# A token-mixing kernel with a second layer norm: a masked copy goes to GpSimd, a normalisation to ScalarE, and the hand-written order of four engines is set anew

## The chip, the cores and the metric

The kernel runs on one core of a Trainium2 chip. That core has five engines with a queue each: TensorE (PE: matmuls, with a separate row PEld for the weight loads that run ahead of them), VectorE (DVE), ScalarE (ACT), GpSimd (POOL), and SyncE (SP), which here only issues DMAs. An engine works its own program in order, and waits at semaphores for the others. The metric is the device time of one whole execution in microseconds (us), as the median of the runs.

## The reference

Input `x` is 2 sequences of 4096 tokens with 512 channels, in float32. What is computed, cut to what matters:

```python
h = layernorm(x)
xx = shift(h) - h                          # the token before, minus this one
lo = tanh((h + xx * time_maa_x) @ maa_w1.T)          # "low rank"
xrg, xwa, xk, xv = h + xx * (lo_g @ maa_w2[g] + time_maa[g])
r, k, v = xrg @ Wr.T, xk @ Wk.T, xv @ Wv.T           # 512x512 projections
g = tanh(xrg @ gate_w1.T) @ gate_w2
w, a, ma, mk, kk = ...                     # gates of low rank, kk normalised per head
s = 0                                      # 16 heads, a 32x32 state each
for t in tokens:
    s = s * w[t] + (s @ kk[t]) * b[t] + v[t] * k[t]
    y[t] = s @ r[t]
y = headnorm(y) * ln_w + ln_b + (r * k * time_faaaa).sum() * v
x = x + (y * g) @ Wo.T
x2n = layernorm(x)                         # the second normalisation
q = round(x2n / (max|x2n| / 127))          # int8 rows
out = x + (q @ weight_q.T) * x_scale * weight_scale + bias
```

## The kernel before, in words

The tokens are cut into 64 tiles of 64 tokens of both sequences (128 rows). The recurrence over tokens is solved in chunks of 32: per head and chunk, score matrices of 32x32 are built, and a triangular system is inverted by powers (three rounds named `power(m, 0..2)`), then by two halves: `half_inverse` and `inverse`, whose result is the tile `tx`. With `tx` two chunks are solved one after the other (`from_values`, `from_state`, `solve_step`, `from_solutions`, with c = 0 in `bank_b` and c = 1 in `bank_a`).

The work is a software pipeline written out by hand. Every engine has a function `tile_step(i)` which lists, in a fixed order, what that engine does for four tiles at a time: `mix` for tile j = i+1 (first layer norm, shift, low rank, mixed inputs), `project` for tile i (keys, values, queries, gates), `solve` for tile m = i-1 (the recurrence), and `finish` for tile n = i-2 (head norm, output projection, second layer norm, quantising, feed-forward). No scheduler or pool decides anything: the order of lines in `tile_step` is the order on the engine, and semaphores (named by the producer, `v_` DVE, `a_` ACT, `g_` GpSimd, `p_` TensorE) tie the engines together. There are 66 steps, of which 63 both project one tile and solve another.

Names that matter below. On TensorE: `queries` (`bank<-xm_rg,w_r`) and `values` (`bank<-xm_v,w_v`), each a projection cut into four blocks of 4 matmuls, which the profile counts as 8 since a float32 matmul is run in two passes; `transposed_input` (`ident,xn`); `low_rank` (`mix,w_maa`); `project_out` (`w_o,yc`), also in four blocks; `power` (`bank_a<-first/pw`, 64 small matmuls on 32x32 tiles); `half_inverse` and `inverse` (the same with narrower right-hand sides); `from_values` (`km,vT`), on 64x64 tiles. On DVE: `half_inverse(m)` ends with the masked copy `tx<-pw,mask_half`; `inverse(m)` adds TensorE's result to it; `shift_mix(j)` makes `xx` and `mix` from the transposed input `xT`, which ACT copies out of PSUM in `front_transposed`; `quantiser(n)` begins with the second normalisation `x2n<-xres,mv,rs`. Of GpSimd's work the multiplications in `weighted_bonus`, `kept_keys`, `undecayed` and `bonus_values`, and the power of -1/2 (`rs`) in `norm2_rstd`, stand near the change.

Of the kernel before, what the change touches and what calls it, by code (L numbers as in the profile page):

```python
# [34 lines left out]
def rwkv_ffn_kernel(nc, a, out):  # L35
# [11 lines left out]
    with ExitStack() as ctx:  # L47
# [73 lines left out]
        def in_spare(groups):  # L121
# [34 lines left out]
        bn2, mv2, rs2 = sb("bn2", [P, 6]), sb("mv2", [P, 2]), sb("rs2", [P, 2])  # L156
        x2n = sb("x2n", [P, C])
# [34 lines left out]
        (v_pl, v_vraw, v_vsum, v_vT, v_qkT, v_rk, v_blT, v_klT, v_pm, v_km, v_e, v_ptT, v_sums, v_te, v_t4, v_tx,  # L192
         v_teT, v_t, v_rhs, v_state, v_rkv) = (
            sem(f"v_{n}") for n in
            "pl vraw vsum vT qkT rk blT klT pm km e ptT sums te t4 tx teT t rhs state rkv".split())
        a_pw, a_u, a_y, a_g, a_b2, a_k2, a_vT2 = (sem(f"a_{n}") for n in "pw u y g b2 k2 vT2".split())
        g_qk, g_qkf, g_rkv = (sem(f"g_{n}") for n in "qk qkf rkv".split())
# [3 lines left out]
        (v_ysqT, v_yvar, v_yrs, v_z1, v_yg, v_x2, v_st2, v_x2n, v_qs, v_q1, v_q2, v_ffn) = (  # L201
            sem(f"v_{n}") for n in "ysqT yvar yrs z1 yg x2 st2 x2n qs q1 q2 ffn".split())
        a_ysq, a_lnv, a_rstd, a_affine, a_qT = (sem(f"a_{n}") for n in "ysq lnv rstd affine qT".split())
# [75 lines left out]
        @block.sync  # L279
        def _(sp):  # L280
            def load_x(i):
                sp.wait_ge(a_xn, count(i, 1, 0))
                for b in range(B):
                    sp.dma_start(xin[b * TB:(b + 1) * TB, :], x_tiles[i, b]).then_inc(x_loaded, 16)

            def load_residual(m):
                sp.wait_ge(stored, count(m, 32, 0))
                sp.wait_ge(g_x2b, count(m, 1, 0))
                sp.wait_ge(v_x2n, count(m, 1, 0))
# [36 lines left out]
        def _(pool):  # L326
# [134 lines left out]
            def tile_step(i, mix=True, project=True, solve=True, finish=True):  # L461
                j, m, n = i + 1, i - 1, i - 2
                if mix:
                    norm_rstd(j)
                if project:
                    kept_keys(i)
                if solve:
                    decayed_state(m)
                    bonus(m)
                if finish:  # L470
                    add_bonus(n)
                if solve:
                    weighted_bonus(m)
                if project:
                    undecayed(i)
                if solve:
                    bonus_values(m)
                if finish:
                    norm2_rstd(n)
                    residual_bias(n)  # L480
                if mix:
                    mixed_inputs(j, XWA, XRG)
                if finish:
                    finish_rows(n)
# [17 lines left out]
        def _(act):  # L502
# [156 lines left out]

            def quantised(n):  # L660
                act.wait_ge(p_qT, count(n, 1, 1))
                run(qT[:], fb[1][:].bitcast(BF16)[:, 0:W].rearrange("p (k t) -> p k t", k=KB),
                    ACT.Copy).then_inc(a_qT, 1)

            def tile_step(i, mix=True, project=True, solve=True, finish=True):
# [8 lines left out]
                if project:  # L674
                    ma_gate(i)
                    a_gate(i)
                    squares(i)
                    mk_gate(i)
# [7 lines left out]
                if solve:  # L686
                    power(m, 1)
                if finish:
                    head_affine(n)
                if solve:  # L690
                    value_pairs(m)
                if project:
                    log_sigmoid(i)
                if mix:
                    normalised(j)
                if solve:
                    power(m, 2)
# [4 lines left out]
                if project:  # L702
                    log_squares(i)
                    exp_tables()
                    key_decay(i)
                    exponentials(i)
                if mix:
                    low_rank(j)
                if project:
                    queries(i)  # L710
                if solve:
                    solution(m, 0)
                    output_gate(m)
                if project:
                    gate_hidden(i)
                if solve:
                    solution(m, 1)
                if finish:
                    quantised(n)
                if mix:  # L720
                    hidden(j, 0)
                    hidden(j, 1)
                if solve:
                    outputs(m, 0)
                    outputs(m, 1)
# [14 lines left out]
        def _(dve):  # L740
# [133 lines left out]
            def half_inverse(m):  # L874
# [7 lines left out]
                dve.wait_ge(v_t4, count(m, 1, 1))  # L882
                tt(tx[:].rearrange("p g (a t) -> p g a t", a=2),
                   pw[:, :, 1, HALF:].unsqueeze(2).to_broadcast([P, G, 2, HALF]),
                   mask_half[:].rearrange("p (a t) -> p a t", a=2).unsqueeze(1).to_broadcast([P, G, 2, HALF]),
                   ALU.mult).then_inc(v_tx, 1)
# [84 lines left out]
            def tile_step(i, mix=True, project=True, solve=True, finish=True):  # L971
# [9 lines left out]
                if solve:  # L981
                    token_major_values(m)
                    enter(m)
                    power(m, 0)
                if project:
                    key_norm(i)
                if mix:
                    norm_shift(j)
                if solve:
                    token_major_keys(m)  # L990
                if finish:
                    head_norm(n)
                if solve:
                    power(m, 1)
                    scores_k(m)
                if finish:
                    gate_heads(n)
                if project:
                    decay_sums(i)
                if solve:  # L1000
                    bonus_rows(m)
# [5 lines left out]
                if solve:  # L1007
                    half_inverse(m)
                    inverse(m)
                if project:  # L1010
                    removal_directions(i)
                if solve:
                    right_hand_sides(m, 0)
                    bonus_sums(m)
                if finish:
                    residual(n)
                if solve:
# [12 lines left out]
                if solve:  # L1030
                    bonus(m)
                if mix:
# [5 lines left out]
                if project:  # L1038
                    decayed(i)
                if finish:  # L1040
# [22 lines left out]
        def _(pe):  # L1063
# [228 lines left out]
            def tile_step(i, mix=True, project=True, solve=True, finish=True):  # L1292
# [11 lines left out]
                if project:  # L1304
                    queries(i, [0])
                    values(i, [0])
                    decay_gate(i)
                if solve:
                    power(m, 1)
                if project:  # L1310
                    queries(i, [1])
                    values(i, [1])
                    values(i, [2])
                    values(i, [3])
                    queries(i, [2])
                if solve:
                    power(m, 2)
                    from_values(m, 0)
                if mix:
                    transposed_input(j)  # L1320
                if project:
                    queries(i, [3])
# [4 lines left out]
                if finish:  # L1327
                    project_out(n, [1])
                    project_out(n, [2])
                if mix:  # L1330
                    low_rank(j)
                if solve:
# [21 lines left out]
                if mix:  # L1354
                    hidden(j, 0)
                    hidden(j, 1)
                if finish:
                    feed_forward(n)

# [52 lines left out]
```

## Time and profile before

| | |
|---|---|
| median of 3 runs | 3238.7 us (3226.87 to 3242.51) |
| the profiled execution's own time | 3244.0 us |
| its span in the trace | 3242.2 us |
| PE busy | 93% of the span |
| PEld busy | 83% |
| DVE busy | 81% |
| ACT busy | 61% |
| POOL busy | 39% |
| share of PE in the chain that ended last | 92% |

The span is the time from the first to the last instruction in the trace; 1.8 us of the execution lie around it. Busy is the share of the span in which an engine had an instruction in work; matmuls overlap each other, so PE's share alone does not say how near it is to its limit. The chain that ended last is followed back from the last instruction to whatever released each step.

### The profile page before, as it was taken

The numbers are of one execution on the slowest core, as the hardware profiler recorded it, in microseconds if no ns is written. First come the engines' busy times: TensorE is split into PE (matmuls) and PEld (weight loads), VectorE is DVE, ScalarE is ACT, GpSimd is POOL, SyncE is SP. The second block draws the span as 40 slices with busy tenths as digits, with TensorE's granted clock in tenths as the row PEclk, the third lists the DMA queues.
The fourth block names the chain that finished last, engine by engine and source line by source line (L and its number), as shares of the span: only waits on it lengthen the run. The fifth ranks groups of instructions, "written<-read, shape, count | busy, mean of one in ns | idle before, by whom it ended". The sixth has DMA issues, their size and how long they took to land.

```text
span 3242.2 us, 182735 instructions
## 1 busy us (share of the span) xinstructions
PE 3029.1 (93%) x84224; PEld 2675.6 (83%) x84224; DVE 2626.5 (81%) x5443; ACT 1974.8 (61%) x3519; POOL 1270.6 (39%) x1161
## 2 busy tenths in 40 slices
PE   6999999999999999999999999999999999999996
PEld 5888888888888888888888888888888888888884
DVE  4788888888888888887888888887888878888875
ACT  3575675665665665755656656656567566566563
POOL 4334334334334344343344343443433434433332
PEclk9999999999999999999999999999999999999998
DMA  3000000000000000000000000000000000000000
GB/s 118 10 23 20 17 23 19 18 20 18 22 20 17 23 20 17 23 20 17 22 20 19 20 17 23 20 17 23 20 17 23 20 17 20 20 20 20 16 17 19
DMA packets 39380, 70.47 MB, mean 22 GB/s; under 512 B 9812, under 2 KB 10836, under 8 KB 38616
## 3 DMA queue, kind: packets, MB, share of 16 engines
q1 hardware_dynamic: 38616, 58.77, 6.8%
q8 instruction: 664, 10.88, 1.4%
q14 instruction: 100, 0.82, 0.1%
HBM read 41.97 MB, written 16.78 MB: 18 GB/s over the span
## 4 chain that ended last, share of the span: by engine, by line
PE 92%; issue 3%; ACT 2%; DVE 2%; POOL 0%; POOLq 0%; ACTq 0%; DVEq 0%
PE bank L1070 30%; PE bank_a L1209 12%; PE bank L1273 8%; PE bank_a L1187 4%; PE bank L1077 4%; PE bank_b L1187 4%; PE bank_b L1244 3%; PE bank_b L1237 3%; PE bank_a L1237 3%; PE bank_a L1244 3%; PE bank_a L1217 2%; PE bank_a L1225 2%; PE bank L1123 2%; PE bank_a L1263 2%; PE bank_b L1263 2%
## 5 line engine op out<-in xcount | busy, mean ns | idle before, releaser
L504 ACT ACT_TABLE_LOAD x383 | 491.4, 1283 | 19.1 <-DVE shift L761 12.2
L1070 PE MATMUL bank<-xm_rg,w_r 128*128 128x128 f32 x2048 | 285.4, 282 | 4.3 <-issue 3.5
L504 ACT ACTIVATE u<-bank_a,parity 128x256 f32<-128x256 f32 x128 | 53.7, 471 | 386.7 <-PE bank_a L1253 386.7
L1209 PE MATMUL bank_a<-pw,w_ffn_int 32*32 32x64 f32 x16384 | 264.6, 216 | 22.0 <-issue 17.2
L1273 PE MATMUL bank<-w_o,yc 128*128 128x512 f32 x512 | 268.9, 626 | 11.0 <-DVE yc L744 9.3
L1209 PEld LDWEIGHTS bank_a<-pw,w_ffn_int 32*32 32x32 f32 x16384 | 239.6, 106 | 41.7 <-issue 21.3
L1070 PEld LDWEIGHTS bank<-xm_rg,w_r 128*128 128x128 f32 x2048 | 248.9, 191 | 26.8 <-issue 15.9
L504 ACT ACTIVATE u<-bank_b,parity 128x256 f32<-128x256 f32 x128 | 53.8, 471 | 342.3 <-PE bank_b L1253 342.3
L1070 PEld LDWEIGHTS bank<-xm_k,w_k 128*128 128x128 f32 x2048 | 241.2, 194 | 12.5 <-issue 3.8
L1070 PE MATMUL bank<-xm_v,w_v 128*128 128x128 f32 x2048 | 250.2, 275 | 0.0
L1070 PE MATMUL bank<-xm_k,w_k 128*128 128x128 f32 x2048 | 241.7, 277 | 3.5 <-issue 3.5
L1070 PEld LDWEIGHTS bank<-xm_v,w_v 128*128 128x128 f32 x2048 | 239.3, 192 | 0.3
L870 DVE STREAM_TRANSPOSE w_ffn_int<-bank_a 128x512 f32<-128x512 f32 x192 | 137.3, 715 | 90.9 <-ACT pw L504 90.3
L399 POOL TENSOR_TENSOR yc<-yc,rkv 128x512 f32<-128x512 f32 x64 | 82.0, 1281 | 321.7 <-ACT yc L504 321.7
L396 POOL TENSOR_TENSOR kept<-ga,gma 128x512 f32<-128x512 f32 x64 | 81.5, 1274 | 311.6 <-ACT ga L504 311.6
L396 POOL TENSOR_TENSOR kkp<-kk,pinv 128x512 f32<-128x512 f32 x64 | 75.3, 1177 | 288.8 <-DVE kk L744 288.8
L396 POOL TENSOR_TENSOR kmod<-kraw,pinv 128x512 f32<-128x512 f32 x64 | 77.1, 1205 | 261.1 <-ACT pinv L504 261.1
L744 DVE TENSOR_TENSOR first<-bank_a,mask_b 128x1024 f32<-128x1024 f32 x64 | 78.4, 1225 | 106.7 <-PE bank_a L1187 106.7
L399 POOL TENSOR_TENSOR o_sb<-o_sb,x2b 128x512 f32<-128x512 f32 x64 | 81.5, 1274 | 199.3 <-DVE o_sb L968 199.3
L1209 PE MATMUL bank_a<-first,w_ffn_int 32*32 32x64 f32 x8192 | 135.0, 215 | 18.7 <-issue 17.7
L396 POOL TENSOR_TENSOR qkT<-qkT,faaaa_T 128x512 f32<-128x512 f32 x64 | 81.4, 1272 | 166.2 <-DVE qkT L914 166.2
L399 POOL TENSOR_TENSOR xm_wa<-xm_wa,xT 128x512 f32<-128x512 f32 x64 | 89.5, 1399 | 128.4 <-DVE xm_wa L779 128.4
(204 smaller groups left out, 8540.4 us busy)
## 6 DMA issues: line engine op xcount, KB each, us to landing
xin<-in_x SPq DMA_DIRECT2D x128, 128.0 KB, 2.7
xres<-in_x SPq DMA_DIRECT2D x128, 128.0 KB
out<-o_sb SPq DMA_DIRECT2D x128, 128.0 KB, 2.4
w_ffn_int<-in_weight_q SPq DMA_DIRECT2D x1, 2048.0 KB, 10.8
w_k<-in_Wk SPq DMA_DIRECT2D x1, 1024.0 KB
w_r<-in_Wr SPq DMA_DIRECT2D x1, 1024.0 KB
w_v<-in_Wv SPq DMA_DIRECT2D x1, 1024.0 KB
w_o<-in_Wo SPq DMA_DIRECT2D x1, 1024.0 KB, 14.2
```

The costliest lines, as they stand in the source:

```text
L396: return nc.gpsimd.tensor_tensor(out_, in0, in1, ALU.mult)
L399: return nc.gpsimd.tensor_tensor(out_, in0, in1, ALU.add)
L504: return nc.scalar.activation(out_, in_, func, **kw)
L870: V.transpose(pt, pairs(bank_a)[:, :, 0, :]).then_inc(v_ptT, 1)
L1070: ins = mm(bank[:, o * n:(o + 1) * n], weights[:, k, o * P:(o + 1) * P], x[:, k].rearrange("p b t -> p (b t)"), start=(k == 0), stop=(k == ...
L1077: ins = mm(bank[:, o * TOK:(o + 1) * TOK], weights[:, o * P:(o + 1) * P], hidden[:], start=True, stop=True)
L1187: ins = mm(bank[q, 64 * n:64 * n + 64], both(keys_[q, g]), both(aq[q, g, 0:2]), start=True, stop=True)
L1209: ins = mm(bank_a[q, 64 * n:64 * n + 64], pt[q, g, :], source[q, g, 0:2].rearrange("p j t -> p (j t)"), start=True, stop=True)
L1237: mm(bank[q, 4 * CHUNK * j:4 * CHUNK * j + 3 * CHUNK], both(vT2[q, g]), km[q, g].rearrange("p j t -> p (j t)"), start=(j % 4 == 0), stop=F ...
L1244: ins = mm(bank[q, 4 * CHUNK * j:4 * CHUNK * j + 3 * CHUNK], both(s_old2[q, j]), aq[q, g].rearrange("p j t -> p (j t)"), start=False, stop ...
L1263: ins = mm(bank[q, 4 * CHUNK * j + CHUNK:4 * CHUNK * j + 3 * CHUNK], both(u2[q, j]), first[q, g, 2:4].rearrange("p j t -> p (j t)"), start ...
L1273: ins = mm(fb[0][:], yc[:, k * TOK:(k + 1) * TOK], w_o[:, k, :], start=(k == 0), stop=(k == KB - 1))
```

## The change

Two operations change engines. The masked copy `tx<-pw,mask_half` leaves DVE's `half_inverse` and becomes GpSimd's `spread_inverse(m)`; DVE's `inverse` now waits for `g_tx`. The second normalisation leaves DVE's `quantiser` and becomes ACT's `normalised_rows(n)`, as scale times x plus shift; DVE computes the shift (128x1) in a new `norm2_shift(n)`, which waits for GpSimd's `g_rs2`. The other part is the order in `tile_step` of all four engines.

```diff
+            def spread_inverse(m):                                   # GpSimd
+                pool.wait_ge(v_t4, count(m, 1, 1))
+                pool.wait_ge(p_u, count(m, NC, 0))
+                nc.gpsimd.tensor_tensor(tx[:].rearrange("p g (a t) -> p g a t", a=2),
+                   pw[:, :, 1, HALF:].unsqueeze(2).to_broadcast([P, G, 2, HALF]),
+                   mask_half[:].rearrange("p (a t) -> p a t", a=2).unsqueeze(1).to_broadcast([P, G, 2, HALF]),
+                   ALU.mult).then_inc(g_tx, 1)
...
+            def normalised_rows(n):                                  # ScalarE
+                act.wait_ge(v_shift2, count(n, 1, 1))
+                act.wait_ge(v_q2, count(n, 1, 0))
+                run(x2n[:], xres[:], ACT.Identity, scale=rs2[:, 1:2], bias=shift2[:]).then_inc(a_x2n, 1)
...
             def inverse(m):                                          # VectorE
                 dve.wait_ge(p_t, count(m, 1, 1))
-                dve.wait_ge(v_tx, count(m, 1, 1))
+                dve.wait_ge(g_tx, count(m, 1, 1))
...
+            def norm2_shift(n):
+                dve.wait_ge(g_rs2, count(n, 1, 1))
+                dve.wait_ge(a_x2n, count(n, 1, 0))
+                V.scalar_tensor_tensor(shift2[:], mv2[:, 0:1], -1.0, rs2[:, 1:2], ALU.mult,
+                                       ALU.mult).then_inc(v_shift2, 1)
+
             def quantiser(n):
-                dve.wait_ge(g_rs2, count(n, 1, 1))
-                V.tensor_scalar(x2n[:], xres[:], mv2[:, 0:1], rs2[:, 1:2], ALU.subtract, ALU.mult).then_inc(v_x2n, 1)
-                dve.wait_ge(v_x2n, count(n, 1, 1))
+                dve.wait_ge(a_x2n, count(n, 1, 1))
...
                 if finish:                                           # VectorE, tile_step
                     residual(n)
+                    norm2_shift(n)
                 if solve:
                     update_state(m, 0)
...
                 if solve:                                            # TensorE, tile_step
                     power(m, 2)
+                if project:
+                    queries(i, [2])
+                    queries(i, [3])
+                if solve:
                     from_values(m, 0)
                 if mix:
                     transposed_input(j)
-                if project:
-                    queries(i, [3])
                 if finish:
                     project_out(n, [0])
                 if solve:
                     half_inverse(m)
                 if finish:
                     project_out(n, [1])
+                if mix:
+                    low_rank(j)
+                if finish:
                     project_out(n, [2])
-                if mix:
-                    low_rank(j)
```

TensorE, from the last part of `values` ahead of `power(m, 2)` to `inverse(m)`. Before (x4 is one block of `queries` or `values`):

```order
L1070 MATMUL bank<-xm_v,w_v 128x128 x12
L1070 MATMUL bank<-xm_rg,w_r 128x128 x4
L1209 MATMUL bank_a<-pw,w_ffn_int 32x64 x64
L1237 MATMUL bank_b<-km,vT 64x96 x16
L1104 MATMUL bank<-ident,xn 128x128 x4
L1070 MATMUL bank<-xm_rg,w_r 128x128 x4
L1273 MATMUL bank<-w_o,yc 128x512
L1217 MATMUL bank_a<-pw,w_ffn_int 32x32 x64
L1273 MATMUL bank<-w_o,yc 128x512 x2
L1070 MATMUL bank<-mix,w_maa 128x128 x4
L1225 MATMUL bank_a<-pw,w_ffn_int 32x16 x64
```

The same place now:

```order
L1088 MATMUL bank<-xm_v,w_v 128x128 x4
L1227 MATMUL bank_a<-pw,w_ffn_int 32x64 x64
L1088 MATMUL bank<-xm_rg,w_r 128x128 x8
L1255 MATMUL bank_b<-km,vT 64x96 x16
L1122 MATMUL bank<-ident,xn 128x128 x4
L1291 MATMUL bank<-w_o,yc 128x512
L1235 MATMUL bank_a<-pw,w_ffn_int 32x32 x64
L1291 MATMUL bank<-w_o,yc 128x512
L1088 MATMUL bank<-mix,w_maa 128x128 x4
L1291 MATMUL bank<-w_o,yc 128x512
L1243 MATMUL bank_a<-pw,w_ffn_int 32x16 x64
```

Two blocks of `queries` now stand together behind `power(m, 2)`, where one had stood ahead of it and one behind `transposed_input`; `low_rank` is one block of `project_out` earlier behind `half_inverse`.

ACT, from `power(m, 1)` (`pw<-bank_a`) to the copy of `xT`. Before:

```order
L504 ACTIVATE pw<-bank_a 128x16x32
L504 ACTIVATE yc<-yc,ln_b,ln_w 128x128 x4
L504 ACTIVATE vT<-vT,parity 128x16x32 x2
L504 ACT_TABLE_LOAD
L504 ACTIVATE lnsig<-sig,sig_floor 128x512
L504 ACTIVATE xn<-xin,shift,rs 128x512
L504 ACTIVATE pw<-bank_a 128x16x32
L504 ACTIVATE val<-bank 128x512
L504 ACTIVATE xT<-xT 128x8
L504 ACTIVATE xT<-bank 128x512
L504 ACTIVATE kss<-kss 128x16
L643 ACT_TABLE_LOAD
```

And now:

```order
L514 ACTIVATE pw<-bank_a 128x16x32
L514 ACTIVATE vT<-vT,parity 128x16x32 x2
L514 ACTIVATE yc<-yc,ln_b,ln_w 128x128 x4
L653 ACT_TABLE_LOAD
L514 ACTIVATE lnsig<-sig,sig_floor 128x512
L514 ACTIVATE kss<-kss 128x16
L514 ACTIVATE pw<-bank_a 128x16x32
L514 ACTIVATE xn<-xin,shift,rs 128x512
L514 ACTIVATE val<-bank 128x512
L514 ACTIVATE xT<-xT 128x8
L514 ACTIVATE xT<-bank 128x512
```

One table load serves the logarithms and the exponentials now, so a step has one load fewer; `xn` moved behind `pw`.

GpSimd, from `kept_keys` to the first of `mixed_inputs`. Before:

```order
L396 TENSOR_TENSOR kept<-ga,gma 128x512
L396 TENSOR_TENSOR s_old<-state,plast 128x512
L396 TENSOR_TENSOR w_ffn_int<-aq,kt 128x512
L399 TENSOR_TENSOR yc<-yc,rkv 128x512
L396 TENSOR_TENSOR qkT<-qkT,faaaa_T 128x512
L396 TENSOR_TENSOR kmod<-kraw,pinv 128x512
L396 TENSOR_TENSOR kkp<-kk,pinv 128x512
L396 TENSOR_TENSOR kmod<-kmod,z 128x512
L396 TENSOR_TENSOR qkT<-w_ffn_int,rk 128x512
L451 TENSOR_TENSOR rs<-rs,minus_half 128x1
L399 TENSOR_TENSOR x2b<-xres,ffn_bias 128x512
L399 TENSOR_TENSOR xm_wa<-xm_wa,xT 128x512
```

And now:

```order
L397 TENSOR_TENSOR qkT<-qkT,faaaa_T 128x512
L397 TENSOR_TENSOR kept<-ga,gma 128x512
L400 TENSOR_TENSOR yc<-yc,rkv 128x512
L397 TENSOR_TENSOR s_old<-state,plast 128x512
L429 TENSOR_TENSOR tx<-pw,mask_half 128x512
L397 TENSOR_TENSOR qkT<-w_ffn_int,rk 128x512
L397 TENSOR_TENSOR kmod<-kraw,pinv 128x512
L397 TENSOR_TENSOR kkp<-kk,pinv 128x512
L397 TENSOR_TENSOR kmod<-kmod,z 128x512
L460 TENSOR_TENSOR rs<-rs,minus_half 128x1
L400 TENSOR_TENSOR xm_wa<-xm_wa,xT 128x512
```

`tx` stands behind `s_old`, `bonus_values` (`qkT<-w_ffn_int,rk`) moved ahead of the three multiplications of `undecayed`, and `x2b` left this place for the end of the step. DVE's `bonus_sums`, for which `bonus_values` waits, went ahead of its `right_hand_sides(m, 0)`; its `bonus_rows` went ahead of `head_norm`, and its two transposes of `token_major_keys` behind `scores_k`.

## Rows read from the trace of the kernel before

**Rows 1.** The page: each engine's busy us, share of the span, instructions.

```profile
PE 3029.1 (93%) x84224; PEld 2675.6 (83%) x84224; DVE 2626.5 (81%) x5443; ACT 1974.8 (61%) x3519; POOL 1270.6 (39%) x1161
```

**Rows 2.** Busy time and instructions of each engine, 200 to 3000 us.

```profile
200.00:3000.00 2800.00, 2667.45 (x74608) 2360.95 (x74603) 2323.20 (x4823) 1751.82 (x3122) 1112.91 (x965) 1.00 0.08 20
```

**Rows 3.** Waits of PE, 200 to 3000 us: total, times, longest.

```profile
PE bank_a L1253 <- DVE rhs_sb L896: 36.7, 57, 0.6
PE bank_a L1263 <- ACT u L504: 31.0, 57, 0.6
...
PE bank_a L1217 <- issue: 10.0, 14, 1.0
...
PE bank_b L1237 <- issue: 1.7, 5, 0.4
```

**Rows 4.** Timeline of PE: start, length, what; idle before it in brackets.

```profile
1606.35 1.16 PE L1070 MATMUL bank<-xm_rg,w_r 128*128 128x128 f32 x8
...
1617.72 1.54 PE L1237 MATMUL bank_b<-km,vT 64*64 64x96 f32 x32
1619.19 0.66 PE L1104 MATMUL bank<-ident,xn 128*128 128x128 f32 x4
1619.68 1.06 PE L1070 MATMUL bank<-xm_rg,w_r 128*128 128x128 f32 x8
1620.58 1.02 PE L1273 MATMUL bank<-w_o,yc 128*128 128x512 f32 x2
1621.53 1.29 PE L1217 MATMUL bank_a<-pw,w_ffn_int 32*32 32x32 f32 x128
1622.75 1.98 PE L1273 MATMUL bank<-w_o,yc 128*128 128x512 f32 x4
1624.57 1.05 PE L1070 MATMUL bank<-mix,w_maa 128*128 128x128 f32 x8
...
1631.04 1.16 PE L1070 MATMUL bank<-xm_rg,w_gate 128*128 128x128 f32 x8
1632.13 1.15 PE L1263 MATMUL bank_b<-first,u 64*64 64x64 f32 x32
...
1653.89 1.16 PE L1070 MATMUL bank<-xm_rg,w_r 128*128 128x128 f32 x8
```

**Rows 5.** Timeline of DVE in the same step.

```profile
1621.71 0.69 DVE L744 TENSOR_TENSOR xx<-xT 128x512 f32<-128x512 f32 x1
1622.44 1.14 DVE L769 SCALAR_TENSOR_TENSOR mix<-xx,maa_x,xT 128x128 f32<-128x128 f32 x4
...
1633.32 0.45 DVE L900 STREAM_TRANSPOSE state<-bank_b 128x256 f32<-128x256 f32 x1 [1.19 <-PE bank_b L1263]
...
1642.71 1.67 DVE L822 SCALAR_TENSOR_TENSOR kt<-kept,kmod 128x512 f32<-128x512 f32 x1
```

**Rows 6.** Timeline of ACT: the copy of the transposed input.

```profile
1619.94 0.60 ACT L504 ACTIVATE xT<-bank 128x512 f32<-128x512 f32 x1 [0.27 <-PE bank L1104]
```

**Rows 7.** Timeline of GpSimd in the same step.

```profile
1642.28 1.55 POOL L399 TENSOR_TENSOR xm_rg<-xm_rg,xT 128x512 f32<-128x512 f32 x1 [0.35 <-DVE xm_rg L779]
```

**Rows 8.** Groups of instructions by line: busy us, mean ns, idle before them.

```profile
L504 ACT ACT_TABLE_LOAD x383 | 491.4, 1283 | 19.1 <-DVE shift L761 12.2
L396 POOL TENSOR_TENSOR kmod<-kraw,pinv 128x512 f32<-128x512 f32 x64 | 77.1, 1205 | 261.1 <-ACT pinv L504 261.1
L504 ACT ACTIVATE xn<-xin,shift,rs 128x512 f32<-128x512 f32 x64 | 51.1, 799 | 0.0
L744 DVE TENSOR_TENSOR tx<-pw,mask_half 128x512 f32<-128x512 f32 x64 | 48.8, 762 | 0.0
L744 DVE TENSOR_TENSOR tx<-bank_a,tx 128x256 f32<-128x256 f32 x64 | 27.2, 424 | 125.0 <-PE bank_a L1225 125.0
L952 DVE TENSOR_SCALAR x2n<-xres,mv,rs 128x512 f32<-128x512 f32 x64 | 35.1, 549 | 0.7 <-POOL rs L451 0.7
```

More of the change, by code:

```diff
@@ L462, in tile_step @@
                 j, m, n = i + 1, i - 1, i - 2
+                if solve:
+                    bonus(m)
                 if mix:
                     norm_rstd(j)
+                if solve:
+                    weighted_bonus(m)
                 if project:
                     kept_keys(i)
-                if solve:
-                    decayed_state(m)
-                    bonus(m)
                 if finish:
@@ L472, in tile_step @@
                 if solve:
-                    weighted_bonus(m)
+                    decayed_state(m)
+                    spread_inverse(m)
+                    bonus_values(m)
                 if project:
                     undecayed(i)
-                if solve:
-                    bonus_values(m)
                 if finish:
                     norm2_rstd(n)
-                    residual_bias(n)
                 if mix:
@@ L483, in tile_step @@
                 if finish:
+                    residual_bias(n)
                     finish_rows(n)
@@ L687, in tile_step @@
                     power(m, 1)
+                    value_pairs(m)
                 if finish:
                     head_affine(n)
+                if project:
+                    exp_tables()
+                    log_sigmoid(i)
+                    log_squares(i)
                 if solve:
-                    value_pairs(m)
-                if project:
-                    log_sigmoid(i)
+                    power(m, 2)
                 if mix:
                     normalised(j)
-                if solve:
-                    power(m, 2)
                 if project:
@@ L702, in tile_step @@
                 if project:
-                    log_squares(i)
-                    exp_tables()
+                    exponentials(i)
                     key_decay(i)
-                    exponentials(i)
+                    queries(i)
                 if mix:
                     low_rank(j)
-                if project:
-                    queries(i)
                 if solve:
+                    output_gate(m)
                     solution(m, 0)
-                    output_gate(m)
                 if project:
                     gate_hidden(i)
+                if finish:
+                    normalised_rows(n)
                 if solve:
@@ L721, in tile_step @@
                     hidden(j, 0)
+                if solve:
+                    outputs(m, 0)
+                if mix:
                     hidden(j, 1)
                 if solve:
-                    outputs(m, 0)
                     outputs(m, 1)
@@ L1000, in tile_step @@
                 if solve:
-                    bonus_rows(m)
+                    scores_k(m)
+                if mix:
+                    norm_shift(j)
+                if solve:
+                    enter(m)
+                    token_major_keys(m)
+                if finish:
+                    gate_heads(n)
+                if solve:
                     power(m, 2)
@@ L1012, in tile_step @@
                 if solve:
+                    inverse(m)
+                    bonus_sums(m)
                     right_hand_sides(m, 0)
-                    bonus_sums(m)
                 if finish:
                     residual(n)
+                    norm2_shift(n)
                 if solve:
@@ L1029, in tile_step @@
                     mixed_inputs(j, XK, XV)
-                if solve:
-                    bonus(m)
-                if mix:
                     mixed_inputs(j, XRG, XRG)
@@ L1039, in tile_step @@
                     decayed(i)
+                if solve:
+                    bonus(m)
                 if finish:
@@ L1304, in tile_step @@
                 if project:
-                    queries(i, [0])
                     values(i, [0])
                     decay_gate(i)
+                    queries(i, [0])
                 if solve:
@@ L1310, in tile_step @@
                 if project:
-                    queries(i, [1])
                     values(i, [1])
                     values(i, [2])
+                    queries(i, [1])
                     values(i, [3])
-                    queries(i, [2])
                 if solve:
                     power(m, 2)
+                if project:
+                    queries(i, [2])
+                    queries(i, [3])
+                if solve:
                     from_values(m, 0)
@@ L1328, in tile_step @@
                     project_out(n, [1])
-                    project_out(n, [2])
                 if mix:
                     low_rank(j)
+                if finish:
+                    project_out(n, [2])
                 if solve:
@@ L1355, in tile_step @@
                     hidden(j, 0)
-                    hidden(j, 1)
                 if finish:
                     feed_forward(n)
+                if mix:
+                    hidden(j, 1)
             pe.wait_ge(const_done, 1)
```

33 lines of the change are left out of this document (11 added, 22 removed).

## The prediction

> **What bounds the kernel now.** I read the page first. TensorE is busy for 93% of the span, VectorE for 81%, ScalarE for 61% and GpSimd for 39% [rows 1]. VectorE is what the change relieves, so the question is whether TensorE ever waits for VectorE. The windows view gives the mean step: 74608 matmuls in 2800 us, at 84224 / 64 = 1316 a tile, is 56.7 steps, or 49.4 us each [rows 1, 2]. The waits of TensorE in the same window come next [rows 3]. Only two engines release it, in every step and always by the same amount: VectorE's `rhs_sb` (36.7 / 57 = 0.64 us, longest 0.6) and ScalarE's `u` (31.0 / 57 = 0.54 us, longest 0.6). Both belong to one chain without slack: from_state, transpose on VectorE, solve, copy on ScalarE, from_solutions. A wait whose longest is its mean is the length of a hand-over and not an engine that comes late. The other rows in that view are "issue", in which TensorE waited for no semaphore.
>
> The timeline of one step shows the rest. From one first block of `queries` to the next it takes 1653.89 - 1606.35 = 47.54 us, with TensorE's groups end to end [rows 4]. So a step without an issue wait takes 47.5 us, of which 1.2 are the two hand-overs, and the mean of 49.4 holds some 1.9 us of issue waits. TensorE's own work sets the time. Nothing taken off another engine shortens a step unless it shortens those two hand-overs, and whatever its new order adds to TensorE shows at full price.
>
> **The change part by part.**
>
> *The masked copy.* VectorE loses `tx<-pw,mask_half`, 0.76 us a step [rows 8]. It stood ahead of `tx<-bank_a`, before which VectorE idled 125.0 / 64 = 1.95 us for TensorE's `inverse` [rows 8]. It was in a shadow, so nothing is gained. On GpSimd no row shows a masked copy; the nearest is a plain 128x512 multiplication, 1.21 us [rows 8]. It begins when VectorE's `t4` is done, and must end before the sum, which comes at least 0.76 + 1.95 = 2.7 us later, since TensorE's `inverse` does; 1.5 us are spare. I take nothing for it. If that cover were gone, each 0.1 us would be 6 us over the 63 steps.
>
> *The second normalisation.* VectorE loses 0.55 us, ScalarE gains a pass like `xn`, 0.80 us, and loses one table load of 1.28 us [rows 8]. ScalarE idles in that place for several microseconds, and the pass is done before `u` of chunk 1 is due. VectorE gains a 128x1 operation that waits for GpSimd's `rs`, and behind that wait stand `state`, `s_old`, `xm_wa` and the second `rhs_sb`, the last on TensorE's chain. GpSimd's queue ahead of `rs` is now `bonus_values` and three multiplications of 1.2 us each in a row, 4.8 us from the sum of the bonus on. VectorE reaches the new wait with 1.19 us in hand, the idle time that it had before `state` [rows 5]. By this reckoning the shift is ready at about the same time as TensorE's result for `state`, from 0.4 us before to 0.4 us after. VectorE saves 0.55 us behind it, ahead of `rhs_sb`, so even the late end costs nothing. Zero for this part.
>
> *TensorE's order, a cost.* The float32 projections run in groups of 128x128 tiles, the recurrence in 32x32 and 64x64 tiles. A block of 8 matmuls inside a group of 128x128 takes 1620.58 - 1619.68 = 0.90 us from start to start. The block `w_gate`, alone between a 32x32 group and a 64x64 group, takes 1632.13 - 1631.04 = 1.09 us [rows 4]. Going into and out of such a group so costs 0.19 us. Before, `from_values` (`km,vT`) followed `power` directly. Now two blocks of `queries` stand between them, an island with a way in and a way out, and the block behind `ident,xn` that is gone was in the inside of a group. The groups around `values` and around `low_rank` keep their number. That adds 0.19 us in 63 steps, 12 us. The Trainium skill, in TensorEngine Tiling (Array Packing), section Key Properties, says that a change of tiling mode drains TensorE; it gives no figure, and it speaks against this order.
>
> *Issue waits, a gain.* The stretch from `from_values` to `half_inverse` was 1621.53 - 1617.72 = 3.81 us [rows 4], and with a second block of `queries` ahead of it the space between the two dense groups of small matmuls grows to about 4.9 us. Issue waits come in dense groups, and those that end in this stretch are 1.7 us in all at `from_values` and 10.0 at `half_inverse` [rows 3]. The bounds are then 0 (they stay) and -12 us (all go). On the other side the stretch between `power(m, 1)` and `power(m, 2)` loses a block, 0.90 us. I take the middle, -6 us. The Trainium skill, in Runtime: NRT & Kernel Launch, section Instruction fetch mechanics, says that instructions are fetched in blocks of 256 and that this is mostly hidden. By that this term would be zero and the total 6 us higher. The trace does not agree that it is hidden: 1.9 us of the mean step are issue.
>
> *Low rank, a cost.* `transposed_input` now runs 1.9 us later against `power(m, 2)`, and `low_rank` 0.9 us earlier against it. Before, `mix` was ready at 1622.44 + 1.14 = 1623.58 and TensorE took it at 1624.57, so 0.99 us were spare [rows 4, 5]. Now ScalarE's copy of `xT` comes last: it starts 1619.94 - 1619.19 = 0.75 us after `ident,xn` starts and takes 0.60; `xx` takes 1622.44 - 1621.71 = 0.73 and `mix` 1.14 [rows 4 to 6]. With 0.1 for the hand-over to VectorE, my choice, that is 3.32 us. TensorE gets there after `ident,xn` 0.49, one block of `w_o` 0.95, `half_inverse` 1.22 and half of the 1.82 us of two blocks, 0.91, together 3.57 us [rows 4]. The hand-over to TensorE with its weight load takes 0.1 to 0.3. So between 0.15 us spare and 0.05 us late. I take 0.05, which is 3 us over 63 steps.
>
> *All else.* The swaps of gates and of `head_affine` on ScalarE, `x2b` and `bonus` on GpSimd, and `feed_forward` ahead of the second `hidden` move work that other work hides: TensorE waits for none of their results before [rows 3]. At the two ends of the run, where latency counts, ScalarE's pass in place of VectorE's adds some 0.5 us once.
>
> *The sum.* On the profiled execution's own 3244.0 us: +12 - 6 + 3 = 3253 us. The median of the runs is 5.3 us below that execution, so 3248 us there. A measurement of this kernel tells about 0.5% from no change, 16 us.
>
> **The rivals.**
>
> *Slower: `low_rank` waits for VectorE.* For it speaks that the slack goes from 0.99 to about zero, and that VectorE's queue ahead of `xx` gets fuller. GpSimd now multiplies twice in a row (`faaaa_T`, `kept`, each like the 1.2 us of `kmod` [rows 8]) just where VectorE's `head_norm` stands. In the trace VectorE's `kt`, which reads two tiles, took 1.67 us beside GpSimd's `xm_rg`, from 1642.71 to 1644.38, and that one ended at 1643.83 [rows 5, 7]. So it ran in the 0.55 us behind it. If `head_norm` is held for both products, `power(m, 1)` and all that follows on VectorE come up to 1.9 us later. Of this 0.7 us are won back by the transposes that moved behind. It decides from 0.12 us a step on, beyond the forecast. At 0.4 us a step it is 25 us, 3273 us. Against it: VectorE idled in several places of this stretch. The Trainium skill, in SBUF — State Buffer, section Who interferes with whom, says that such an instruction of VectorE and a reading one of GpSimd exclude each other; the row of `kt` agrees.
>
> *Faster: issue waits shrink by more.* They are 1.9 us a step. If the wider spacing took a third of them, 0.6 us, that is -38 in place of -6 us, 3216 us. Against it: only 11.7 us of those on TensorE's row lie in the stretch that changes [rows 3].
>
> *Faster: VectorE was the limit after all.* If the 0.64 and 0.54 us were VectorE's lateness, its relief of 1.3 us a step would take both, 57 x 1.18 = 67 us, for 3181 us. Against it stands that neither wait ever varies [rows 3].
>
> **How the numbers follow.** The forecast has 0.50, and 0.03 more for a change that shows nothing at all. The slower rival has 0.31, the issue waits 0.12, VectorE 0.04. Faster by over 0.5% is then 0.16, within it 0.53, slower 0.31. The two likelier rivals bound the range: 3273 above, and below the forecast with all the bounds on the good side and part of the second rival, 3222.
>
> **What would show it.** On TensorE: the two blocks of `queries` start to start in 1.98 us (0.90 + 1.09), a step without an issue wait of 47.7 us, waits for `rhs_sb` and `u` as before. VectorE's share should fall to about 79%, ScalarE's table loads by 64. If I am wrong upward, the waits view has a row of `low_rank` for `mix`, or of `power` for `pw`. If I am wrong downward, the mean step is under 49 us while the undisturbed one stays at 47.5 or above, or one of the two hand-overs is shorter.

## The result and the profile after

The changed kernel takes 3248.83 us in the median of 11 runs (3246.52 to 3253.46); the kernel before, run beside it, took 3234.57 (3226.81 to 3242.51). The ratio is 1.0048, with a 95% interval of 1.0035 to 1.0061: 11 to 20 us slower. Forecast were 3248 us, with a sum of +9 us; against the runs beside it the difference is +14 to +15 us. That the two totals lie within 1 us is luck: the kernel before was 4 us lower in the runs beside it than in those that the forecast started from (3238.7), and the rise was 5 us more. The two traced executions are 4 us apart (3244.0 and 3248.25 us), since that of the kernel before lay 9 us above its median; so the rows are compared term by term, and not by their totals.

The page after, each engine's busy time (before: [rows 1]):

```profile
PE 3031.2 (93%) x84224; PEld 2663.0 (82%) x84224; DVE 2672.1 (82%) x5379; ACT 1951.0 (60%) x3519; POOL 1381.9 (43%) x1225
```

VectorE lost two operations, together 1.3 us a step, and is busier than before. The waits of TensorE, 200 to 3000 us (before: [rows 3]):

```profile
PE bank_a L1227 <- issue: 46.4, 59, 1.5
PE bank_a L1271 <- DVE rhs_sb L908: 36.7, 57, 0.6
PE bank_a L1281 <- ACT u L514: 31.1, 57, 0.6
PE bank L1088 <- issue: 5.3, 13, 0.6
PE bank_a L1235 <- issue: 3.3, 7, 0.8
PE bank_a L1243 <- issue: 2.5, 3, 1.0
```

Both hand-overs are what they were, to 0.1 us in 57 steps. No row names `mix`, so `low_rank` waits for nothing, and no new releaser has come. TensorE's timeline in one step (before: [rows 4]):

```profile
1611.38 1.16 PE L1088 MATMUL bank<-xm_v,w_v 128*128 128x128 f32 x8
...
1621.86 2.05 PE L1088 MATMUL bank<-xm_rg,w_r 128*128 128x128 f32 x16
1623.84 1.54 PE L1255 MATMUL bank_b<-km,vT 64*64 64x96 f32 x32
...
1659.12 1.16 PE L1088 MATMUL bank<-xm_v,w_v 128*128 128x128 f32 x8
```

The island of two blocks takes 1623.84 - 1621.86 = 1.98 us, as forecast, and the step without an issue wait 1659.12 - 1611.38 = 47.74 us against 47.54 [rows 4]. ScalarE's table loads fell by 64, from 383 to 319 beside the 64 of the other line, as forecast. The groups of VectorE that grew most, and the new one (busy us, mean ns):

```profile
L761 DVE TENSOR_TENSOR aq<-kk,pdec 128x512 f32<-128x512 f32 x64 | 86.8, 1357 | 0.0
L761 DVE TENSOR_TENSOR yc<-y_sb,gn_rstd 128x512 f32<-128x512 f32 x64 | 79.9, 1249 | 2.2
L965 DVE SCALAR_TENSOR_TENSOR shift<-mv,rs 128x1 f32<-128x1 f32 x64 | 13.4, 209 | 86.6 <-POOL rs L460 86.6
```

The same two of the kernel before:

```profile
L744 DVE TENSOR_TENSOR yc<-y_sb,gn_rstd 128x512 f32<-128x512 f32 x64 | 44.3, 692 | 2.2
L744 DVE TENSOR_TENSOR aq<-kk,pdec 128x512 f32<-128x512 f32 x64 | 41.2, 644 | 0.0
```

Both read two tiles in SBUF. Beside `yc`, GpSimd now multiplies for `weighted_bonus` and `kept_keys`; beside `aq`, it adds `x2b`. That is 35.6 + 45.6 = 81 us more on VectorE, nearly the 84 us (48.8 + 35.1) that it had lost [rows 8]. `bt` went from 44.0 to 61.3 us and the `shift` of the first normalisation from 11.0 to 33.9, and the new `shift` above takes 13.4. As TensorE's waits show, all of this lies in slack.

The start of the run is where the two traces part most. The chain that ended last, start, length and what, first the kernel before:

```profile
44.44 0.60 ACT xT L504
...
71.53 1.92 PE bank_a L1209 x128
```

and after:

```profile
36.87 0.69 DVE bn L768
37.90 0.70 DVE kk L761
38.74 2.05 PE bank L1088 x8
...
50.17 0.61 ACT xT L514
...
78.43 1.92 PE bank_a L1227 x128
```

In the step that projects tile 0, TensorE's first `values` needs VectorE's `kk`, and VectorE makes `kk` behind the statistics `bn` of tile 1, whose input comes by DMA among the weights. Before, a block of `queries`, which does not need `kk`, stood first. TensorE's waits in the first 130 us after the change have it in one row:

```profile
PE bank L1088 <- DVE kk L761: 3.4, 1, 3.4
```

The copy of `xT` comes 5.7 us later and the first `power` 6.9 us later. But the kernel before was traced in its earliest start. In the traces of the ten kernels below with the old first step, the first `power` lies between 72.3 and 76.4 us, and TensorE waits for `kk` there as well, 0.6 to 2.6 us; the input's DMA landed later in most of them. The mean of all eleven is 74.0 us, that of the three kernels with the new step on the other engines 77.9. So the new start costs some 4 us, an estimate from fourteen traces, and not 6.9.

### The profile page after: what moved, and what is told of

It reads as the page before. It is cut to its first block, busy times and chain, and to the rows that moved or that the text cites. A ratio compares the mean times of both kernels' runs of the same rounds, so it can differ in the third digit from the quotient of the medians.

```text
span 3246.5 us, 182927 instructions
## 1 busy us (share of the span) xinstructions
PE 3031.2 (93%) x84224; PEld 2663.0 (82%) x84224; DVE 2672.1 (82%) x5379; ACT 1951.0 (60%) x3519; POOL 1381.9 (43%) x1225
## 4 chain that ended last, share of the span: by engine, by line
PE 91%; issue 3%; ACT 2%; DVE 2%; SPq 1%; DMA 0%; POOL 0%; POOLq 0%; ACTq 0%; DVEq 0%
PE bank L1088 30%; PE bank_a L1227 12%; PE bank L1291 8%; PE bank_a L1205 4%; PE bank L1095 4%; PE bank_b L1205 4%; PE bank_b L1262 3%; PE bank_a L1255 3%; PE bank_b L1255 3%; PE bank_a L1262 3%; PE bank_a L1235 2%; PE bank_a L1243 2%; PE bank_a L1281 2%; PE bank_b L1281 2%; PE bank L1141 2%
## 5 line engine op out<-in xcount | busy, mean ns | idle before, releaser
L1291 PE MATMUL bank<-w_o,yc 128*128 128x512 f32 x512 | 277.7, 624 | 11.5 <-DVE yc L761 10.1
L1088 PE MATMUL bank<-xm_v,w_v 128*128 128x128 f32 x2048 | 275.8, 282 | 5.8 <-DVE kk L761 3.4
L1088 PE MATMUL bank<-xm_rg,w_r 128*128 128x128 f32 x2048 | 268.6, 279 | 3.6 <-issue 3.6
L429 POOL TENSOR_TENSOR tx<-pw,mask_half 128x512 f32<-128x512 f32 x64 | 81.2, 1269 | 422.1 <-DVE pw L761 422.1
L514 ACT ACTIVATE gate<-bank 128x512 f32<-128x512 f32 x64 | 38.2, 597 | 353.6 <-PE bank L1095 353.6
L400 POOL TENSOR_TENSOR xm_wa<-xm_wa,xT 128x512 f32<-128x512 f32 x64 | 75.4, 1178 | 192.9 <-DVE xm_wa L796 192.9
L400 POOL TENSOR_TENSOR xm_k<-xm_k,xT 128x512 f32<-128x512 f32 x64 | 75.4, 1179 | 171.6 <-DVE xm_k L796 171.6
L397 POOL TENSOR_TENSOR qkT<-w_ffn_int,rk 128x512 f32<-128x512 f32 x64 | 67.0, 1047 | 172.2 <-DVE rk L922 172.2
L1227 PEld LDWEIGHTS bank_a<-first,w_ffn_int 32*32 32x32 f32 x8192 | 118.1, 105 | 21.1 <-issue 13.3
```

Of the source, the lines that this page charges most:

```text
L397: return nc.gpsimd.tensor_tensor(out_, in0, in1, ALU.mult)
L400: return nc.gpsimd.tensor_tensor(out_, in0, in1, ALU.add)
L514: return nc.scalar.activation(out_, in_, func, **kw)
L1088: ins = mm(bank[:, o * n:(o + 1) * n], weights[:, k, o * P:(o + 1) * P], x[:, k].rearrange("p b t -> p (b t)"), start=(k == 0), stop=(k == ...
L1227: ins = mm(bank_a[q, 64 * n:64 * n + 64], pt[q, g, :], source[q, g, 0:2].rearrange("p j t -> p (j t)"), start=True, stop=True)
L1291: ins = mm(fb[0][:], yc[:, k * TOK:(k + 1) * TOK], w_o[:, k, :], start=(k == 0), stop=(k == KB - 1))
```

## The experiments

Each was timed in five rounds beside the kernel before; ratios are to that kernel, with 95% intervals, and 0.001 is 3.2 us. The kernel before took 3232.5, 3237.3 and 3242.7 us in the three sittings (the first four experiments, the next four, the last four), so only ratios can be compared between them, and not the times that the expectations name.

**The island alone.** In the kernel before:

```diff
-                    queries(i, [2])
                 if solve:
                     power(m, 2)
+                if project:
+                    queries(i, [2])
+                    queries(i, [3])
+                if solve:
                     from_values(m, 0)
...
-                if project:
-                    queries(i, [3])
```

> The kernel before with one edit: the last two blocks of queries stand together behind power(m, 2), nothing else. If the island of 128x128 matmuls between two groups of small ones is the cost, each of 63 steps gets 0.19 to 0.21 us longer: 12 to 13 us, less up to 6 for issue waits, so 3241 to 3248 us against 3234.6. In the trace the two blocks take 1.98 us from start to start and the undisturbed step 47.7 us. If the other engines' orders or the two moved operations cost the time, this kernel stays at 3234.6 us.

Measured 1.0066 (1.0054 to 1.0078), 21 us. Its timeline shows 1.98 us again:

```profile
1625.84 2.05 PE L1070 MATMUL bank<-xm_rg,w_r 128*128 128x128 f32 x16
1627.82 1.54 PE L1237 MATMUL bank_b<-km,vT 64*64 64x96 f32 x32
```

That is 0.2 us by 63 steps, 12.6 us. Issue waits did not fall: TensorE's rows of them add up to 73.6 us against 63.7 before. The island costs what was forecast, and the gain set against it was a loss here: 9.9 us more in 57 steps, 11 in 63. The two make 24 us, of which 21 were measured.

**The island taken out of the kernel after**, the same edit backwards.

> The kernel after with one edit: queries block 2 is back ahead of power(m, 2) and block 3 behind transposed_input, so that from_values follows power directly. Island theory: 3248.8 less 7 to 13, so 3236 to 3242 us, the rest being the start of the run. Rival (other engines' orders cost it): stays at 3248.8 us.

Measured 1.0040 (1.0028 to 1.0052): 3 us less than the kernel after, within the intervals. The theory wanted 7 to 13. Its issue rows add up to 66.1 us, against 62.6 in the kernel after. So in the full new order the island brought part of its price back in issue waits. The mean granted clock of this kernel's runs was also lower, 0.992 against 0.993, which by the reckoning further down hides another 3 to 4 us. What is left, 13 us above the kernel before, is the start and something besides.

**The two operations alone.** The kernel before with the functions `spread_inverse`, `normalised_rows` and `norm2_shift` of the change, placed in the old orders:

```diff
                     weighted_bonus(m)                 # GpSimd
+                    spread_inverse(m)
...
                     gate_hidden(i)                    # ScalarE
+                if finish:
+                    normalised_rows(n)
...
                     residual(n)                       # VectorE
+                    norm2_shift(n)
```

> The kernel before with the two operations on their new engines, and every other line of the four orders as before (the masked copy stands behind weighted_bonus on GpSimd, the normalisation behind gate_hidden on ScalarE, the shift behind residual on VectorE). My theory: both were in the shadow of other work, so 3234.6 us within 3. Rival, VectorE matters: 0.76 + 0.55 us less a step on it gives up to 67 us less. Rival, the new waits cost (VectorE behind GpSimd's rs): 6 us for each 0.1 us a step.

Measured 1.0005 (0.9995 to 1.0016). Moving them gives nothing and takes nothing. The 128x1 `shift` behind GpSimd's `rs` takes 1.22 us in the mean here, beside `x2b`, and TensorE's wait for `rhs_sb` is 36.7 us all the same.

**TensorE's old order in the kernel after.** Its `tile_step` on TensorE is that of before.

> The kernel after with TensorE's tile_step as before; the orders of VectorE, ScalarE and GpSimd and the moved operations stay. If TensorE's order is the whole cost, island and start of the run, this is back at 3234.6 us within 4. If the other engines' orders cost part, that part stays: up to 3248.8 us.

Measured 1.0046 (1.0034 to 1.0059). It does not tell what it was made for, since the orders belong together: ScalarE now makes `gma` last of the gates, and `queries`, first again on TensorE, waits for it.

```profile
PE bank L1088 <- ACT gma L514: 16.7, 32, 0.5
```

One thing it does tell: TensorE does not wait for `kk` at the start of this kernel, and its first `power` is at 78.0 us nonetheless, as late as after the change. So the wait for `kk` is not the whole of what the new start costs.

**The start in the old order.** In the kernel after, the step that projects tile 0 runs through a `first_step` on all four engines, which is the old `tile_step`.

```diff
-            tile_step(0, solve=False, finish=False)
+            first_step(0, solve=False, finish=False)
```

> The kernel after, with the one step that projects tile 0 (and solves none) in the order of before on all four engines. In the traces the copy of xT in that step starts at 50.17 us after and 44.44 before, and the first power at 78.1 and 71.5. If the start of the run is a cost of its own, 4 to 7 us come back: 3242 to 3245 us against 3248.8. If the lost time is made up later (the next step took 47.4 us after and 50.3 before), it stays at 3248.8 us.

Measured 1.0024 (1.0013 to 1.0035): 0.0024 less than the kernel after, 8 us of its 15, with an error of some 5. Its first `power` starts at 74.65 us, 3.8 us earlier than after the change. The trace bears out the lower end of what was expected, and about half of the 8 us. The rest is not shown to be the start's: this kernel's runs had a higher mean granted clock than those of the kernel before beside them (0.9936 against 0.9924).

**Both.**

> Both: the start in the old order and queries block 2 and 3 back around power(m, 2), the rest as after. Island and start as the whole cost: 3233 us within 4, as before. If something else in the new orders costs, what lies above 3236 us is that.

Measured 1.0022 (1.0009 to 1.0035), 7 us. Taking the island out again gave nothing on top that the intervals can tell. About 7 us of the new orders (3 to 11 by the interval) belong to neither. They are no added work of TensorE: with each of its groups at the usual length (the first quartile over the steps from 200 to 3000 us), a step adds up to 47.53 us here and in the kernel before, and to 47.73 in the kernel after. Its issue rows add up to 66.7 us against 63.7; the rest stays open.

**An island less.** The other way round in the kernel before: the fourth block of `project_out` stands ahead of `inverse`, beside the third.

```diff
-                if solve:
-                    inverse(m)
                 if finish:
                     project_out(n, [3])
                 if solve:
+                    inverse(m)
                     from_state(m, 0)
```

> The kernel before with one edit: the fourth block of project_out goes ahead of inverse(m), beside the third, so that inverse and from_state follow each other. If each way into and out of a group of 128x128 matmuls costs 0.19 to 0.2 us, an island less in 62 steps gives back 12 us: 3220 us against 3232.5. Rival: inverse comes 0.95 us later and its sum on VectorE is late for solve_step(m, 0), or denser groups draw more issue waits; then 3232 us or above.

Measured 1.0099 (1.0083 to 1.0115): 32 us slower. TensorE's waits have grown in one row:

```profile
PE bank_a L1253 <- DVE rhs_sb L896: 61.9, 57, 1.4
```

VectorE's `s_old`, ns at least, in the median and at most:

```profile
L744 DVE TENSOR_TENSOR s_old<-state,plast x64: 691/1468/1711, 106.1 to 3232.1; 128x512 f32<-128x512 f32 x64
```

In the kernel before the same row is:

```profile
L744 DVE TENSOR_TENSOR s_old<-state,plast x64: 691/762/774, 104.4 to 3205.4; 128x512 f32<-128x512 f32 x64
```

and one such moment of the joined kernel on VectorE's timeline,

```profile
1644.56 1.63 DVE L744 TENSOR_TENSOR s_old<-state,plast 128x512 f32<-128x512 f32 x1
```

and on GpSimd's:

```profile
1644.34 1.30 POOL L399 TENSOR_TENSOR x2b<-xres,ffn_bias 128x512 f32<-128x512 f32 x1
```

`s_old` started 0.2 us behind `x2b` and ended 0.55 us after it. In the kernel before, `x2b` ran from 1632.73 to 1634.02 and `s_old` from 1633.81: they brush by 0.2 us, and `s_old` is held for 0.07. The denser order moved them onto each other. A second cost came with it: the mean granted clock of TensorE is 0.987 against 0.992 in the kernel before. TensorE had waited longer in each step; that the longer wait brought the clock down was not tested by itself, but all four joined kernels in which TensorE waits longer have it (0.986 to 0.989 in the mean of their runs), and the two without it do not (0.992 and 0.994). At the lower of its two levels (1.2 in place of 2.4 GHz) half of a stretch's time is lost, so 0.005 of 3269 us are 16 us. The reckoning is -12 for the island that is gone, +28 for the wait (25.2 us in 57 steps, scaled to 63), +16 for the clock: +32, as measured.

**The same in the kernel after**, with the old start and without the island.

> The last one, with the fourth block of project_out ahead of inverse(m) as well. Island theory: 12 us below e7_old_start_no_island, some 3221 us, below both kernels. Rival (issue waits take it back): no difference to it.

Measured 1.0008 (1.0000 to 1.0017), 5 us below the one without the joined block, where 12 were expected. Here `x2b` stands at the end of GpSimd's step, `s_old` takes 0.69 us throughout, and the wait for `rhs_sb` stays at 37.8 us. So one part of the new orders has a worth, which shows once TensorE is ahead.

**Which part of the change makes room for the joined block.** Four kernels of before with the joined block, the first with both operations moved:

> e3_ops_only (both operations on their new engines, old orders) with the fourth block of project_out ahead of inverse(m), the edit that cost 33 us in e6_joined. There TensorE's wait for rhs_sb of chunk 1 rose from 36.7 to 61.9 us and VectorE's s_old took 1.47 us (median) in place of 0.76, beside GpSimd's x2b. Theory, VectorE's load counts once TensorE is ahead: 0.55 us less on VectorE between s_old and rhs_sb takes most of the extra wait away, 3222 to 3235 us. Rival, only the collision counts and the moved operations do nothing for it: about 3265 us.

Measured 1.0087 (1.0073 to 1.0101), 28 us, near the time that its rival named; the rows are below.

> e6_joined with the second normalisation alone on ScalarE; the masked copy stays on VectorE. If the normalisation is what gives VectorE room ahead of rhs_sb, this equals e9_ops_joined, 3222 to 3235 us. If not, 3265 us.

Measured 1.0068 (1.0056 to 1.0081). TensorE waits for `rhs_sb` for 47.6 us, nearly as in the first of the four, so what differs there from the joined kernel is the moved normalisation's doing.

> e6_joined with the masked copy alone on GpSimd. VectorE saves 0.76 us in front of inverse, where it idles 2 us for TensorE: no gain on the late rhs_sb, so 3265 to 3272 us as e6_joined. If VectorE's whole load is what counts, it gets a good part of it back: below 3250 us.

Measured 1.0113 (1.0099 to 1.0128), 37 us; the time of 3278.9 us lies above the range expected. The collision is there as before, with `s_old` at 1.55 us in the median and a wait for `rhs_sb` of 62.9 us in 56 steps, and the mean granted clock of its runs is 0.986, the lowest of all.

> e6_joined with one more edit: GpSimd's x2b (residual_bias) behind mixed_inputs, as in the kernel after; no operation changes its engine. If VectorE's s_old is late because GpSimd reads SBUF beside it, s_old is back at 0.76 us, the wait for rhs_sb at 36.7 us in 57 steps, and the joined block gives its 12 us: 3220 to 3230 us. If the collision is not the cause, 3265 us or more.

Its edit on GpSimd, beside the joined block:

```diff
                     norm2_rstd(n)
-                    residual_bias(n)
                 if mix:
                     mixed_inputs(j, XWA, XRG)
                 if finish:
+                    residual_bias(n)
                     finish_rows(n)
```

Measured 0.9958 (0.9944 to 0.9972): 14 us faster than the kernel before, where 12 were expected, and the only one of all that is faster. Of the 14, some 4 go with a mean granted clock of 0.994 against 0.993. Its row in TensorE's waits:

```profile
PE bank_a L1253 <- DVE rhs_sb L896: 36.6, 57, 0.6
```

and VectorE's `s_old` in ns:

```profile
L744 DVE TENSOR_TENSOR s_old<-state,plast x64: 691/692/693, 107.7 to 3189.9; 128x512 f32<-128x512 f32 x64
```

So the collision is the cause of the joined kernel's loss, and VectorE's load is not. My theory for the first two fell. With both operations moved, `s_old` takes 0.69 us as well, but TensorE's waits have these rows:

```profile
PE bank_a L1270 <- DVE rhs_sb L908: 48.0, 57, 0.9
...
PE bank_a L1261 <- DVE s_old L761: 5.5, 24, 0.3
```

and VectorE's timeline this one, ahead of `state`:

```profile
1643.18 1.22 DVE L965 SCALAR_TENSOR_TENSOR shift<-mv,rs 128x1 f32<-128x1 f32 x1 [1.36 <-POOL rs L460]
```

The wait that the moved normalisation brings holds VectorE for 1.36 us, and the 128x1 operation behind it takes 1.22 us, against 0.21 in the mean of the kernel after, where `x2b` stands elsewhere. One hold took the place of another. The two waits make 16.8 us, 19 over 63 steps. The profiled execution was the quickest of its five, with a clock of 0.990; the mean of the five is 0.987 against 0.993 for the kernel before beside them, which is 18 us. With the -12 of the island the reckoning gives 25 us for the first of the four, and 28 were measured.

## Why the prediction was right, point by point

*What bounds the kernel.* Right. TensorE's own work sets the step, and the moved operations alone changed nothing (1.0005).

*The masked copy and the second normalisation at nothing.* Right in this kernel, for the reasons given. GpSimd's copy takes 1.27 us where 1.21 was taken. The relief of VectorE was overrated: its busy share rose, from 81 to 82%, where 79% was forecast. VectorE's operations that are held beside GpSimd's work in its new places grew by more than the two that left had cost. That cost no time, since TensorE came later everywhere.

*The island, +12 us.* Right in what it adds to TensorE's work: 1.98 us, 47.74 us a step, 63 times 0.2. The rows put the price of a change of tile mode at 0.1 us each way, since a block takes 0.90 us inside a group and 1.09 alone [rows 4]. The Trainium skill says in TensorEngine Tiling (Array Packing), section Key Properties, that a change of mode drains TensorE. The trace shows the time that a change costs, and not the drain itself. The kernel that lost an island without a new wait was 14 us faster.

*Issue waits, -6 us.* Wrong in its argument; the size, -1 us, lies within its bounds of 0 and -12, and is 5 us off the middle that was taken. At `half_inverse` and `inverse` the rows fell from 10.0 and 11.0 to 3.3 and 2.5 us; at `power` they rose from 31.5 to 46.4 us. All rows of TensorE together went from 63.7 to 62.6 us. I had named the stretch between `power(m, 1)` and `power(m, 2)` that gets shorter, and then given it no number. It took back nearly what the other gave. The trace shows how an order moves these waits and hardly makes fewer: counted along all of TensorE's instructions that the trace holds, weight loads included, each of the 88 issue waits of over 0.25 us in this window before, and of the 86 after, stands at the 193rd or 194th place in its run of 256. The prediction also read too much into them. It put the whole 1.9 us between the mean and the undisturbed step down to them, and their rows hold 63.7 us in 56.7 steps, 1.1 us; the rest is in no row of that view. The faster rival, a third of 1.9, would have been more than half of what there was.

*`low_rank`, +3 us.* Too high: it never waits.

*All else, +0.5 us.* This is the term that was put too low. I looked at the swap of `queries` and `values` in the middle of the run, where `kk` is early enough, and not in the first projected step. There `kk` stands behind a DMA, and the new orders cost some 4 us by the first `power` in fourteen traces (8 us by the difference between 1.0048 and 1.0024, itself uncertain by some 5). The wait for `kk` is a part of that, 3.4 us against 0 to 2.6; how the rest divides among the four engines' orders was not tested.

The sum of what was measured is then: island 12.6, issue waits -1, start 4, which is 16 against 15 of the result. Two kernels do not fit it well. Taking the island out gave 3 us and nothing where its rows, less the 3.5 and 5.1 us that the issue rows grew by, make 7 to 9; the intervals, of some 6 us on each difference, reach the first and not quite the second. And 7 us belong to neither island nor start, of which 3 are issue waits. I have not found which of the swaps these belong to, so the sum may fit better than it should.

*The slower rival* had its mechanism right. `head_norm` on VectorE was held for GpSimd's products, 1.25 us in place of 0.69. The Trainium skill has it in SBUF — State Buffer, section Who interferes with whom, that a VectorE instruction with two inputs in SBUF contends with a GpSimd instruction that reads SBUF; the trace agrees. The delay ended in VectorE's idle time and never reached `mix`. The two faster rivals did not come about: both hand-overs are unchanged, and the issue waits moved and did not shrink.

## What to carry to other kernels

When one engine runs without a gap, first count how often it changes its mode of tiles, and join its groups; then look at which other engine's result is now the last one, since two operations that barely touch in the old order may run on top of each other in the new one, and one of them is held. Moving work off an engine that nobody waits for brings nothing, and a wait that such a move adds can cost later. An order made for the steady state must be read once more for the first step, where inputs come by DMA. And a term read off two traces should be checked against all traces of kernels that share that part: here the start shrank from 6.9 to 4 us by it.

## What the runs showed of the hardware that was not expected

A swap of one block on TensorE cost 32 us where it should have given 12, by half a microsecond of waiting in each step (25.2 us in 57) and a clock that fell with it, from a mean of 0.992 to 0.987 of full speed. Moving one addition on GpSimd turned that into a gain of 14 us. A VectorE operation on 128x1 elements took 1.22 us beside a GpSimd addition, and 0.16 us (median) in the kernel after, where GpSimd stood idle beside it; its size says nothing of its time when the other engine reads at the same moment. TensorE's issue waits stand at a fixed place in each run of 256 of its instructions (88 of 88 over 0.25 us before, 86 of 86 after): a new order puts them into other groups.
